# Two layer norms from one pass of statistics in the q, k, v stage of a three-block kernel

## The chip, the cores and the metric

The kernel runs on one core of a Trainium2 chip, in float32. The metric is the device time of one execution, in microseconds. A core has TensorE (matrix products into PSUM, profile name PE, with PEld for its weight loads), VectorE (DVE), ScalarE (ACT), GpSimd (POOL) and SyncE (SP, which here issues DMAs). They run side by side and wait for one another through semaphores.

## The reference

The input is x of 8 x 512 tokens with 128 channels, 4096 tokens in all. Three blocks follow each other, and the first and the third are the same computation:

```python
def _layernorm(x, axis=-1, eps=1e-05):
    m = jnp.mean(x, axis=axis, keepdims=True)
    v = jnp.var(x, axis=axis, keepdims=True)
    return (x - m) / jnp.sqrt(v + eps)

x = x + 0.5 * ffn(_layernorm(x))
x = x + attn(_layernorm(x))            # a recurrence over the tokens
x = x + 0.5 * ffn(_layernorm(x))

def ffn(x):                            # x is already normalized once
    x = x + _msa(_layernorm(x, ln1_w, ln1_b), w_qkv, w_proj)
    return x + _moe_mlp(_layernorm(x, ln2_w, ln2_b), gate_w, gate_b, w1, w2)
```

So at the start of `ffn` two layer norms stand one behind the other: z, the norm of x, which is kept for the residual, and the norm of z, which goes with weight and bias into the product with w_qkv (128 x 384, 16 heads of 8). If x has variance v along its channels, z has mean 0 and variance v / (v + eps).

## The kernel before, in words

`program` (L1949) runs `ffn`, the recurrence, `ffn` again and a last sum. Each `ffn` is four stages, one after another with a barrier of all engines between them: the q, k, v stage (`qkv_phase`, L290), attention, projection (with the second norm and the choice of experts) and experts.

The q, k, v stage works on 8 slices (SL) of 512 tokens; a slice is 4 tiles (ST) of 128 tokens by 128 channels, tokens on the partitions. `pipeline` (L75) lays the slices over each other: in step j an engine does part 0 for slice j, part 1 for slice j-1, and so on up to j-3. Steps 0 to 5 are written out, steps 6 and 7 are one turn of a hardware loop with the slice number in a register, steps 8 to 10 drain. Each engine's order is that in which its `step` lists the parts. Buffers come in pairs, by the parity of the slice.

For one slice:

- VectorE, `lna.center` (L132 to L140): sum over the channels (L134), mean (L136), x minus mean (L140). ScalarE, `squares` (L144): the squares of that. VectorE, `variance` (L151, L153): their sum, then scale and eps. GpSimd, `scale` (L159, L165): the power -0.5, then the multiply that writes z into `z_all`.
- The same four parts again, `lnb`, on z, one step later; GpSimd's multiply writes `zn`.
- TensorE transposes `zn` (L430); ScalarE applies weight and bias and writes `hT` (L384).
- TensorE multiplies: q and k (L420, with the weights stationary) and v (L424).
- ScalarE rounds q and k to a high part (L376), VectorE subtracts it to get the low part (L357), and SyncE stores both parts (L331), 512 KB for q and 512 KB for k per slice. ScalarE copies v into `v_all` (L390).

TensorE's order in a step is: q, k, v of slice j-3, then the transposes of slice j-2. ScalarE's is: high parts of j-3, Squares, `hT` of j-2, copy of v. VectorE's is: center of j, center of j-1, low parts of j-3, variance of j, variance of j-1. In the first `ffn` x is still being loaded, 256 KB a slice; VectorE waits for each.

The projection stage has a norm of another make, on VectorE alone apart from the power: `bn_stats` (L987) and `bn_aggr` (L995) for mean and variance, eps added (L1002), the power on GpSimd (L1140), and one tensor_scalar per tile that subtracts the mean and multiplies (L1008). The recurrence uses the same `LayerNorm` class (`lnr`, `gn`). In the expert stage VectorE copies weights (L1252) from an address that it reads into a register.

## Time and profile before

| | us |
|---|---|
| median of 3 runs | 1597.56 |
| lowest, highest | 1591.68, 1601.63 |
| the profiled execution | 1610.69 |
| its span, first to last instruction | 1608.9 |
| busy: TensorE, VectorE | 1292.8, 1121.5 |
| busy: ScalarE, GpSimd | 877.7, 698.0 |

All rows come from the one profiled execution. "Busy" adds up the durations of an engine's instructions over all stages; an engine that is busy for most of a stage sets its pace there, whatever its share of the whole span. In the timeline a row is a start, a duration, the engine, the line, and in brackets the idle time before it with what ended it; rows with a count (x4) are merged. An instruction may start before the one ahead of it has ended, so the pace of a row of them is read from start to start. Nearly all of the kernel's time lies in two attention stages, two expert stages and the recurrence; the q, k, v stages lie from 6 to 76 us and from 955 to 1028 us of the span.

### The profile page before, as it was taken

The numbers are of one execution on the slowest core, as the hardware profiler recorded it, in microseconds if no ns is written. First come the engines' busy times: TensorE is split into PE (matmuls) and PEld (weight loads), VectorE is DVE, ScalarE is ACT, GpSimd is POOL, SyncE is SP. The second block draws the span as 40 slices with busy tenths as digits, with TensorE's granted clock in tenths as the row PEclk, the third lists the DMA queues.
The fourth block names the chain that finished last, engine by engine and source line by source line (L and its number), as shares of the span: only waits on it lengthen the run. The fifth ranks groups of instructions, "written<-read, shape, count | busy, mean of one in ns | idle before, by whom it ended". The sixth has DMA issues, their size and how long they took to land. (4 is left out here: it accounts for less than half of the span.)

```text
span 1608.9 us, 39937 instructions
## 1 busy us (share of the span) xinstructions
PE 1292.8 (80%) x12720; PEld 732.9 (46%) x12721; DVE 1121.5 (70%) x1736; ACT 877.7 (55%) x1782; POOL 698.0 (43%) x817
## 2 busy tenths in 40 slices
PE   3579999999978397278788745489999999976693
PEld 2324444434458397125445433234444444476593
DVE  7678888888736232758788759588889888463232
ACT  3438888888841153224334314168888888820351
POOL 5433333333336365246566625513333333336462
PEclk9769999999975599589899858689999999965797
DMA  3421433211100121100000002512111111001224
GB/s 111 167 57 43 112 91 78 62 49 48 29 1 30 48 68 51 41 2 2 3 2 2 3 1 105 150 36 51 45 54 46 48 53 45 12 1 43 62 68 117
DMA packets 81641, 81.93 MB, mean 51 GB/s; under 512 B 16265, under 2 KB 53868, under 8 KB 81536
## 3 DMA queue, kind: packets, MB, share of 16 engines
q1 hardware_dynamic: 72704, 70.01, 15.6%
q0 software_dynamic: 4608, 8.44, 1.6%
q10 hardware_dynamic: 4224, 2.10, 0.4%
q8 instruction: 64, 1.05, 0.3%
q14 instruction: 41, 0.34, 0.1%
HBM read 50.56 MB, written 29.93 MB: 50 GB/s over the span
## 5 line engine op out<-in xcount | busy, mean ns | idle before, releaser
L795 DVE TENSOR_REDUCE maxima<-ps 128x2 f32<-128x1024 f32 x512 | 624.1, 1226 | 88.1 <-PE ps L624 83.1
L777 ACT ACTIVATE probs<-ps 128x512 f32<-128x512 f32 x1024 | 553.1, 593 | 87.0 <-PE ps L651 69.7
L624 PE MATMUL ps<-k_stack,q_stack 62*128 62x512 f32 x1024 | 385.8, 476 | 36.6 <-DMA k_stack<-k_split 25.5
L651 PE MATMUL ps<-q_stack,k_stack 64*128 64x512 f32 x1024 | 390.0, 459 | 0.3
L661 PE MATMUL ps<-probs,v_stack 128*32 128x256 f32 x4096 | 327.5, 392 | 1.1 <-ACT probs L777 1.0
L590 POOL TENSOR_TENSOR inv<-o_rows,minus_one 128x16 f32<-128x16 f32 x64 | 186.3, 2911 | 237.4 <-ACT o_rows L758 237.4
L624 PEld LDWEIGHTS ps<-k_stack,q_stack 62*128 62x128 f32 x1024 | 157.7, 193 | 229.7 <-issue 115.9
L651 PEld LDWEIGHTS ps<-q_stack,k_stack 64*128 64x128 f32 x1024 | 159.3, 186 | 17.0 <-issue 7.3
L661 PEld LDWEIGHTS ps<-probs,v_stack 128*32 128x32 f32 x4096 | 80.9, 108 | 171.7 <-issue 112.2
L1275 POOL DMA_INDIRECT expert_out<-yt,number x80 | 78.7, 984 | 69.0 <-issue 44.4
L1233 ACT ACTIVATE xT<-ps,ln_b,ln_w 128x128 f32<-128x128 f32 x80 | 36.6, 458 | 107.2 <-PE ps L1204 105.1
L1252 DVE COPY w_now<-w 128x512 f32 x80 | 34.4, 430 | 77.8 <-issue 41.6
L1210 PE MATMUL ps<-xT,w_now 128*128 128x128 f32 x640 | 88.4, 283 | 0.1
L1217 PE MATMUL ps<-w,hidT 128*128 x640 | 84.9, 276 | 0.0
L1210 PEld LDWEIGHTS ps<-xT,w_now 128*128 128x128 f32 x640 | 80.6, 198 | 0.4 <-issue 0.3
L583 POOL CAST neg_wide<-maxima 128x16 fp32r<-128x16 f32 x64 | 12.7, 198 | 155.1 <-DVE maxima L795 155.1
L1217 PEld LDWEIGHTS ps<-w,hidT 128*128 128x128 f32 x640 | 78.4, 193 | 0.1
L1133 POOL DMA_INDIRECT sorted<-rows,slot x64 | 62.2, 972 | 26.5 <-issue 16.4
L1238 ACT ACTIVATE hidT<-ps 128x512 f32<-128x512 f32 x80 | 47.8, 598 | 36.4 <-PE ps L1210 35.8
L1681 POOL TENSOR_TENSOR r_kx<-r_kx,r_k_factor 128x512 f32<-128x512 f32 x48 | 60.6, 1263 | 13.0 <-PE ps L1859 9.6
L1662 POOL TENSOR_TENSOR r_mixed<-r_shift,zT 128x512 f32<-128x512 f32 x40 | 57.1, 1436 | 19.0 <-DVE r_shift L1538 19.0
L420 PE MATMUL ps<-hT,w_qkv 128*128 128x512 f32 x64 | 44.7, 837 | 17.4 <-ACT hT L384 17.4
(215 smaller groups left out, 1843.8 us busy)
## 6 DMA issues: line engine op xcount, KB each, us to landing
q_stack<-q_split SPq DMA_DIRECT2D x256, 64.0 KB
k_stack<-k_split SPq DMA_DIRECT2D x512, 32.0 KB
q_split<-q_parts SPq DMA_DIRECT2D x16, 512.0 KB, 2.8
k_split<-k_parts SPq DMA_DIRECT2D x16, 512.0 KB, 3.6
xt<-sorted SPq DMA_DIRECT2D x80, 64.5 KB
w<-in_L_ffn_w SPq DMA_DIRECT2D x16, 256.0 KB, 3.0
rows<-expert_out SPq DMA_DIRECT2D x16, 256.0 KB, 3.2
x_all<-in_L_attn_x SPq DMA_DIRECT2D x8, 256.0 KB, 3.0
```

Of the source, the lines that this page charges most:

```text
L590: g_.tensor_tensor(inv[:], o_rows[:, :, :, DK], minus_one[:], ALU.pow).then_inc(inv_ready, 1)
L624: mm = t.matmul(psS[:, h, :], qs[g][score_rows(h), h // 2, u * P:(u + 1) * P], ks[g][score_rows(h), h // 2, :], start=True, stop=True)
L651: t.matmul(ring("e", u, n), ks[g][half(h), h // 2, u * P:(u + 1) * P], qs[g][half(h), h // 2, :], start=True, stop=True).then_inc(e_ready, 1)
L661: last = t.matmul(psO[VW * h:VW * (h + 1), here], vs[g][:, u, h, :], probs[u % 2][:, h, here], start=(u == 0 and part == 0), stop=(u == TP ...
L777: a.activation(probs[u % 2][:, h, :], ring("e", u, n), ACT.Exp, scale=float(DK) ** -0.5).then_inc(e_read, 1)
L795: v.tensor_reduce(maxima[i][:, :, pair, u:u + 1], psS[:, 2 * pair:2 * pair + 2, :], AX_X, ALU.max, negate=True).then_inc(s_read, 1)
L1133: pool.indirect_dma_start(xs, bass.IndirectOffsetOnAxis(ap=slot[:, i:i + 1], axis=0), rows[:, i, :], None).then_inc(scattered, 16)
L1210: last = t.matmul(psH[o][:, c * P:(c + 1) * P], w1_now[o][:, c * P:(c + 1) * P], xT[o][:], start=True, stop=True)
L1217: last = t.matmul(psY[i][:, 0:P], hidT[i][:, c, :], s["w2"][:, ds(second_expert, 1), c, :], start=(c == 0), stop=(c == HC - 1))
L1275: pool.indirect_dma_start(ys, bass.IndirectOffsetOnAxis(ap=number[out_slot][:], axis=0), yt[out_slot][:], None, bounds_check=TOK - 1, oob_ ...
L1662: g.tensor_tensor(mixed[f][:], shift[f % 2][:], x, ALU.add).then_inc(mixed_ready.sem, 1)
L1681: g.tensor_tensor(dst[:].rearrange("p (k m) -> p k m", m=m), src[:].rearrange("p (k m) -> p k m", m=m), k_factor[l][:].rearrange("p n two ...
```

## The change

In `qkv_phase` the two `LayerNorm` objects are replaced. VectorE takes mean and variance of each tile of x with `bn_stats` and `bn_aggr` (`moments_of`). From the variance v it writes two numbers per token: v + eps, and (1 + eps) v + eps^2, which is (v + eps) times (variance of z + eps). GpSimd raises both to the power -0.5 in one instruction of 128x8. One step later (`norm`) VectorE writes, for each of the four tiles, `zn` and `z_all`, both from x, with one tensor_scalar each: subtract the mean, multiply by the scale. ScalarE has no Squares any more, GpSimd no multiplies. TensorE waits for `normed` instead of for GpSimd.

```diff
-        lna = LayerNorm(nc, ctx, "lna", ST, EPS, bufs=2)
-        lnb = LayerNorm(nc, ctx, "lnb", ST, EPS, bufs=2)
+        stats, moments = sb("stats", [P, ST, 6]), sbs("moments", [P, ST, 2])
+        spread, scales, power = sbs("spread", [P, 2, ST]), sbs("scales", [P, 2, ST]), sb("power", [P, 2, ST])
...
+                def moments_of(j, i):
+                    after(vec, moments_made, j, 1)
+                    for q in range(ST):
+                        v.bn_stats(stats[:, q, :], x_all[:, j * ST + q, :] if isinstance(j, int)
+                                   else x_all[:, ds(j * ST + q, 1), :].rearrange("p a c -> p (a c)")).then_inc(stats_made, 1)
+                    after(vec, normed, j, 2)
+                    for q in range(ST):
+                        vec.wait_ge(stats_made, ST * j + q + 1)
+                        last = v.bn_aggr(moments[i][:, q, :], stats[:, q, :])
+                    last.then_inc(moments_made, 1)
+                    vec.wait_ge(moments_made, j + 1)
+                    after(vec, scales_made, j, 2)
+                    v.tensor_scalar(spread[i][:, 0, :], moments[i][:, :, 1], EPS, None, ALU.add)
+                    v.tensor_scalar(spread[i][:, 1, :], moments[i][:, :, 1], 1.0 + EPS, EPS * EPS, ALU.mult,
+                                    ALU.add).then_inc(spread_made, 1)
+
+                def norm(j, i):
+                    vec.wait_ge(scales_made, j + 1)
+                    after(vec, turned, j, 2)
+                    for q in range(ST):
+                        x = x_all[:, ds(j * ST + q, 1), :].rearrange("p a c -> p (a c)")
+                        z = z_all[:, ds(j * ST + q, 1), :].rearrange("p a c -> p (a c)")
+                        v.tensor_scalar(zn[i][:, q, :], x, moments[i][:, q, 0:1], scales[i][:, 1, q:q + 1],
+                                        ALU.subtract, ALU.mult)
+                        last = v.tensor_scalar(z, x, moments[i][:, q, 0:1], scales[i][:, 0, q:q + 1],
+                                               ALU.subtract, ALU.mult)
+                    last.then_inc(normed, 1)
...
-                        lna.center(vec, j, x_all[:, ds(j * ST, ST), :], i)
+                        moments_of(j, i)
                     if present(1):
-                        lna.wait_done(vec, j - 1)
-                        lnb.center(vec, j - 1, z_all[:, ds((j - 1) * ST, ST), :], o)
+                        norm(j - 1, o)
...
-                    if present(0):
-                        lna.variance(vec, j, i)
-                    if present(1):
-                        lnb.variance(vec, j - 1, o)
...
-                    if present(0):
-                        lna.squares(act, j, i)
-                    if present(1):
-                        lnb.squares(act, j - 1, o)
...
                     if present(0):
-                        lna.scale(pool, j, z_all[:, ds(j * ST, ST), :], i)
-                    if present(1):
-                        free = [] if isinstance(j, int) and j < 3 else [(turned, j - 2)]
-                        lnb.scale(pool, j - 1, zn[o][:], o, *free)
+                        pool.wait_ge(spread_made, j + 1)
+                        after(pool, normed, j, 2)
+                        g.tensor_tensor(scales[i][:], spread[i][:], power[:], ALU.pow).then_inc(scales_made, 1)
...
-                        lnb.wait_done(pe, j - 2)
+                        after(pe, normed, j, 2)
```

## Rows read from the trace of the kernel before

**Rows 1.** The page: busy time, share of the span and instructions of each engine.

```profile
PE 1292.8 (80%) x12720; PEld 732.9 (46%) x12721; DVE 1121.5 (70%) x1736; ACT 877.7 (55%) x1782; POOL 698.0 (43%) x817
```

**Rows 2.** Windows, second stage, one step: length, busy time by engine, clock, DMA, GB/s.

```profile
992.28:999.68 7.40, 5.19 (x17) 3.22 (x16) 7.19 (x13) 3.61 (x6) 4.04 (x5) 0.73 0.38 141
```

**Rows 3.** Groups of instructions of the second stage, 955 to 1024 us.

```profile
L165 POOL TENSOR_TENSOR z_all<-lna_centered,lna_rstd 128x512 f32<-128x512 f32 (+1 forms) x8 | 8.4, 1054 | 1.8 <-POOL lna_rstd L159 1.8
...
L136 DVE TENSOR_SCALAR lna_mean<-lna_total 128x4 f32<-128x4 f32 x8 | 6.3, 782 | 0.3
...
L136 DVE TENSOR_SCALAR lnb_mean<-lnb_total 128x4 f32<-128x4 f32 x8 | 5.6, 694 | 0.3
```

**Rows 4.** Timeline of the second stage: start, length, engine, line, operation, idle before.

```profile
955.35 0.69 DVE L134 TENSOR_REDUCE lna_total<-x_all 128x4 f32<-128x512 f32 x1 [1.29 <-PEq L63]
...
968.14 1.12 PE L430 MATMUL ps<-ident,zn 128*128 128x128 f32 x4 [14.80 <-POOL zn L165]
...
970.22 3.78 PE L420 MATMUL ps<-hT,w_qkv 128*128 128x512 f32 x4 [0.96 <-ACT hT L384]
...
976.51 1.98 PE L420 MATMUL ps<-hT,w_qkv 128*128 128x512 f32 x4 [0.87 <-ACT hT L384]
...
978.33 1.05 PE L424 MATMUL ps<-w_qkv,hT 128*128 128x128 f32 x8
...
989.48 0.68 DVE L357 TENSOR_TENSOR q_parts<-ps,q_parts 128x512 fp32r<-128x512 f32 x1
...
990.08 0.68 DVE L357 TENSOR_TENSOR k_parts<-ps,k_parts 128x512 fp32r<-128x512 f32 x1
...
1011.38 0.66 PE L430 MATMUL ps<-ident,zn 128*128 128x128 f32 x4 [2.74 <-POOL zn L165]
...
1012.91 3.78 PE L420 MATMUL ps<-hT,w_qkv 128*128 128x512 f32 x4 [0.87 <-ACT hT L384]
...
1020.01 1.99 PE L420 MATMUL ps<-hT,w_qkv 128*128 128x512 f32 x4 [0.87 <-ACT hT L384]
...
1023.38 0.37 SPq L331 DMA_DIRECT2D k_split<-k_parts  x1
```

**Rows 5.** Timeline of the first stage.

```profile
6.03 0.69 DVE L134 TENSOR_REDUCE lna_total<-x_all 128x4 f32<-128x512 f32 x1 [1.21 <-DMA x_all<-in_L_attn_x]
...
20.73 3.78 PE L420 MATMUL ps<-hT,w_qkv 128*128 128x512 f32 x4 [0.96 <-ACT hT L384]
...
27.30 1.98 PE L420 MATMUL ps<-hT,w_qkv 128*128 128x512 f32 x4 [0.87 <-ACT hT L384]
...
68.56 1.98 PE L420 MATMUL ps<-hT,w_qkv 128*128 128x512 f32 x4 [0.87 <-ACT hT L384]
```

**Rows 6.** Timeline of the projection stage, VectorE and GpSimd.

```profile
473.15 0.87 DVE L987 BATCH_NORM_STATS2 stats<-x 128x6 f32<-128x128 f32 x4
...
474.33 0.17 DVE L1002 TENSOR_SCALAR var<-moments 128x4 f32<-128x4 f32 x1
474.41 0.69 DVE L981 SCALAR_TENSOR_TENSOR x_all<-x,x_all 128x512 f32<-128x512 f32 x1
474.58 1.38 POOL L1140 TENSOR_TENSOR rstd<-var,power 128x4 f32<-128x4 f32 x1 [2.24 <-DVE var L1002]
475.01 1.11 DVE L1008 TENSOR_SCALAR rows<-x,moments,rstd 128x128 f32<-128x128 f32 x4
...
476.04 0.69 DVE L977 TENSOR_TENSOR x<-z_all,ps 128x512 f32<-128x512 f32 x1
```

**Rows 7.** Lines L159 and L1140: durations in ns, min/median/max, first and last start.

```profile
L159 POOL TENSOR_TENSOR gn_rstd<-gn_var,gn_power x8: 1637/1648/1650, 740.5 to 945.6; 128x8 f32<-128x8 f32 x8
...
L1140 POOL TENSOR_TENSOR rstd<-var,power x16: 1281/1404/1499, 471.1 to 1458.5; 128x4 f32<-128x4 f32 x16
```

**Rows 8.** DMA issues of the second stage: count, size, median us to landing.

```profile
k_split<-k_parts SPq DMA_DIRECT2D x8, 512.0 KB, 3.6
```

**Rows 9.** The page, costliest groups: a copy with an address from a register.

```profile
L1252 DVE COPY w_now<-w 128x512 f32 x80 | 34.4, 430 | 77.8 <-issue 41.6
```

More of the change, by code:

```diff
@@ L309, in sem @@
             return ctx.semaphore(name)
-        lna = LayerNorm(nc, ctx, "lna", ST, EPS, bufs=2)
-        lnb = LayerNorm(nc, ctx, "lnb", ST, EPS, bufs=2)
+        stats, moments = sb("stats", [P, ST, 6]), sbs("moments", [P, ST, 2])
+        spread, scales, power = sbs("spread", [P, 2, ST]), sbs("scales", [P, 2, ST]), sb("power", [P, 2, ST])
+        stats_made, moments_made, spread_made, scales_made, normed = (
+            sem("stats_made"), sem("moments_made"), sem("spread_made"), sem("scales_made"), sem("normed"))
+        power_set = sem("power_set")
         zn, hT = sbs("zn", [P, ST, P]), sbs("hT", [P, SW])
@@ L398, in step @@
                 def step(j, i, present):
-                    o = 1 - i
                     if present(0):
-                        lna.scale(pool, j, z_all[:, ds(j * ST, ST), :], i)
-                    if present(1):
-                        free = [] if isinstance(j, int) and j < 3 else [(turned, j - 2)]
-                        lnb.scale(pool, j - 1, zn[o][:], o, *free)
-                lna.start(pool)
-                lnb.start(pool)
+                        pool.wait_ge(spread_made, j + 1)
+                        after(pool, normed, j, 2)
+                        g.tensor_tensor(scales[i][:], spread[i][:], power[:], ALU.pow).then_inc(scales_made, 1)
+                g.memset(power[:], -0.5).then_inc(power_set, 1)
+                pool.wait_ge(power_set, 1)
                 g.memset(v_all[:, :, :, DK:], 1.0).then_inc(ones_set, 1)
-                pipeline(pool, SL, 1, step)
+                pipeline(pool, SL, 0, step)
             @block.tensor
```

## The prediction, made before the changed kernel was run

> **What bounds the kernel now.** I read the page's busy times first: TensorE is busy 80% and VectorE 70% of 1608.9 us, but over stages that differ [rows 1], and the change touches only the q, k, v stage, which runs twice. Of each run I read the timeline: in the second, VectorE's first reduction starts at 955.35 and the last store of k is issued at 1023.38, which is 68.0 us [rows 4]; in the first, VectorE starts at 6.03 and the last slice's q product at 68.56 [rows 5]. The store follows that product by 1023.38 - 1020.01 = 3.37 us, so the first run ends near 71.9. Together that is 134 us, or 8% of the span, and no more than this can be won. Then the windows of one step: in 7.40 us VectorE is busy 7.19, TensorE 5.19, ScalarE 3.61, GpSimd 4.04 [rows 2]. VectorE sets the pace. Some of its time is no work: the means, scalings of 4 numbers per partition, take 782 and 694 ns each, while the like operation on moments takes 0.17 us [rows 3, 6]. They stand beside GpSimd's 128x512 multiplies of 1054 ns [rows 3]. TensorE's 5.19 us are at a granted clock of 0.73 on average, thus partly at 1.2 and partly at 2.4 GHz [rows 2].
>
> **The change, part by part.** Removed per step: from VectorE four reductions, two means, two centerings and two variances (ten instructions), from ScalarE two Squares, from GpSimd one pow and two multiplies. Added on VectorE: four bn_stats, four bn_aggr, two small tensor_scalars, eight 128x128 tensor_scalars. GpSimd keeps one pow, now 128x8. The two subtractions for the low parts of q and k stay.
>
> VectorE's new step, by the projection stage, which does the same in the same shapes. Four bn_stats, four bn_aggr and one small tensor_scalar take 474.41 - 473.15 = 1.26 us, and each further small one 474.41 - 474.33 = 0.08: 1.34 for the moments [rows 6]. Four normalizing tensor_scalars with two per-partition operands take 476.04 - 475.01 = 1.03, eight of them 2.06 [rows 6]. The low parts go 990.08 - 989.48 = 0.60 apart, 1.20 for two [rows 4]. The sum is **4.60 us** against 7.40 [rows 2]. Bounds: if the eight did not overlap at all, 8 x 1.11/4 gives 2.22, and with a full 0.34 each 2.7, so a step is 4.6 to 5.3; below, nothing shown is shorter, and I leave 0.2 for it. I take 4.60, the same form on the same engine.
>
> TensorE is the next limit. Its step has a loop of its own: q, k, v, then the transposes of the next slice, ScalarE's hT, and the next q. At full clock q, k and v take 978.33 + 1.05 - 976.51 = 2.87 us, and from the transposes to the next q 1012.91 - 1011.38 = 1.53: **4.40 us** [rows 4]. At half clock the step is 1020.01 - 1012.91 = 7.10 [rows 4]. Which one holds? Before, the clock falls where TensorE has stood idle for 2 to 3 us a step (2.74 before the transposes at 1011.38, and the products at 1012.91 then take 3.78 instead of 1.98) [rows 4]. After, its idle time is about 0.9 us before q and little else, so I take full clock from the second slice on. One step at 7.10 instead would cost 2.7.
>
> The way in, second run. VectorE's moments of slice 0 end at 955.35 + 1.34 = 956.7; the pow starts 0.25 us after (474.58 - 474.33) [rows 6] and takes 1.65 [rows 7], until 958.6. Meanwhile VectorE does slice 1's moments, then waits 0.6 and writes both results by 960.7. The transposes start there and not at 968.14: 7.35 us earlier. To q(0) it was 970.22 - 968.14 = 2.08 [rows 4], so q(0) is at 962.9. From q(0) to q(1), with the clock still low in q(0), I keep the 976.51 - 970.22 = 6.29 [rows 4]: q(1) at 969.2. Then six steps of 4.40: q(7) at 995.6, and the last store 3.37 later at 998.9 instead of 1023.38: **24.4 us earlier**.
>
> Is VectorE in time? The low parts of slice 0 wait for ScalarE until about 967.5 and end at 968.7, and then each step is 4.60: the normalization of slice 7 ends at 968.7 + 4 x 4.60 + 3.40 = 990.5, and its transposes are due at 995.6 - 1.53 = 994.1. There are 3.6 us to spare, so even 5.3 a step costs under 1 us. The stores: two of 512 KB a step; one of k lands after 3.6 us [rows 8], and its buffer is written again two slices later. The latest, issued about 987.1, has landed at 990.7, and ScalarE wants it near 992.4: hidden, with 1.7 us of cover; without it a step would grow by what is missing. The pow of a slice has a whole step, 4.6 us, before VectorE wants it, and needs 0.25 + 1.65: hidden, with 2.7 us of cover.
>
> First run: the same 7.55 us from VectorE's start to q(0) give 6.03 + 7.55 = 13.6; q(0) to q(1) took 27.30 - 20.73 = 6.57 [rows 5]: 20.2; six steps: 46.6, against 68.56: **22.0 us earlier**. The load of x is no bound: it comes in two slices at a time, in less than a step.
>
> ScalarE loses its Squares, GpSimd its multiplies: neither is on the path, so 0, besides the port. The new waits on VectorE are for its own results (in the 1.26) and for the scales, behind which the low parts and all of the next step are queued; the cover is the 2.7 us. Step 6 and 7 run in a hardware loop, where each of the 12 new instructions takes one or two addresses from registers. The nearest row is a copy with an address from a register, with 41.6 us of issue idle in 80, 0.52 each, with a value load in it [rows 9]; below 0 nothing speaks. I take 0, since VectorE's queue runs ahead, and 0.52 for the range. Fewer semaphores to clear at the end may save some tenths: not counted.
>
> Sum: 24.4 + 22.0 = 46.4. The profiled execution took 1610.69 us (span 1608.9 and 1.8 around it), so it would be 1564.3; it lies 0.8% over the median 1597.56 of the runs, and against that the forecast is **1551.2**.
>
> **The port.** The row: VectorE's small means last until GpSimd's 1.05 us multiply is through, and that goes away with the multiplies [rows 3]. A pow does not do this: in the projection stage it runs from 474.58 for 1.38 us, while VectorE's four tensor_scalars start at 475.01 and keep their pace of 0.26 [rows 6]. The pow in turn varies from 1281 to 1499 ns [rows 7]. The Trainium skill, page "SBUF — State Buffer", section "Who interferes with whom", says that a VectorE tensor_scalar in a two-port mode and a GpSimd instruction lock each other out, the first to issue holding the pair for its whole length. By that rule, the trace agrees for the multiplies and not for the pow, and the new eight tensor_scalars would stand behind the pow in each step; what this would give is the first rival.
>
> **Rivals.**
> (1) The pow holds VectorE back for its 1.65 us a step. VectorE's step is 6.25: the low parts of slice 0 end at 972.0, the normalization of slice 7 at 972.0 + 25.0 + 5.05 = 1002.1, q(7) at 1003.7, 8.1 later than forecast; twice, 16.2: **1567**. For it: the multiplies do hold it. Against it: rows 6. 8%.
> (2) TensorE stays at half clock. q(7) at 962.9 + 7 x 7.10 = 1012.6, and a tail of 3.37 + 3.78 - 1.98 = 5.2: 5.6 us won; in the first run 3.4. Time **1589**. For it: the clock of 0.73 in a step that is 70% busy [rows 2]. Against it: the idle time goes. 6%.
> (3) The register addresses cost 0.52 each: 24 instructions, 12.5 less the 3.6 to spare, 9 a stage: **1569**. 6%.
> (4) The other side: the same place at a higher price. VectorE's sequencer stalls at each of the 24 instructions of the loop. It decides from (24.4 + 3.6)/24 = 1.17 us each; at 1.5 the stage loses 36 - 3.6 - 24.4 = 8 us and the first 10.4: **1616**, slower. For it only that VectorE now issues 20 instructions a step instead of 12; against it that the nearest row has 0.52. 3%. That the change doesn't do what it says has no case: the code leaves no second pass over z.
>
> **How the numbers follow.** The forecast has 77%; its own spread is one slow TensorE step a stage (+5), a faster first step (-4), and the 5 us by which runs differ: 1541 to 1561. The range reaches up to (1) and (3): 1541 to 1571, with (2) and (4) out, 9%, and the tails. A change of 1% (16 us) is about what can be told from none. Faster by more: 0.77 + 0.08 + 0.06 = 0.91; within: 0.06, case (2); slower: 0.03.
>
> **What would show it.** Steps of 4.4 to 4.7 us, with the last k store 43 to 46 us after VectorE's first bn_stats; the first transposes 5.4 us after it; TensorE waiting for hT by 0.9 us a step and hardly for VectorE; clock at 1 from the second slice; no small tensor_scalar above 0.2 us. Wrong would be: tensor_scalars of the norm above 0.5 us beside the pow (1), products of 3.8 us late in the stage (2), VectorE idle by issue in steps 6 and 7 (3, 4), or the attention stages taking longer than before.

## The result, and the profile after

The changed kernel takes 1550.81 us (median of 4 runs, 1547.22 to 1553.92) against 1597.8 for the kernel before (4 runs beside it, 1591.68 to 1601.63): a ratio of 0.9715, 95% interval 0.9682 to 0.9747. The forecast was 1551.2. The profiled execution took 1553.92 us, with a span of 1552.0.

First the page of the changed kernel, busy time, share and instructions of each engine, for [rows 1]:

```profile
PE 1284.2 (83%) x12720; PEld 729.3 (47%) x12721; DVE 1082.9 (70%) x1864; ACT 859.3 (55%) x1750; POOL 659.1 (42%) x767
```

VectorE has 128 instructions more and 39 us less to do, GpSimd 39 us less, ScalarE 18 us less. TensorE does the same work and shows 8.6 us less: in these stages four q and k matmuls take 3.78 us at half clock and 1.98 at full clock, and more of them now run at full clock.

Then one step of the second stage, from one group of `bn_stats` of VectorE to the next, for [rows 2]: length, busy time of PE, PEld, DVE, ACT and POOL with their instructions, granted clock, DMA share, GB/s.

```profile
951.21:955.79 4.58, 3.71 (x18) 2.31 (x17) 4.55 (x21) 2.61 (x5) 1.75 (x1) 1.00 0.59 229
```

A step is 4.58 us instead of 7.40. VectorE is busy for 4.55 of it, TensorE for 3.71, and the granted clock is 1.00, TensorE's 2.4 GHz level, where the step before had 0.73. At full clock both VectorE and TensorE are close to their limits here, which is the point of most experiments below.

The timeline of the second stage, for [rows 4] (start, duration, engine, line, and in brackets the idle time before it and what ended it). The lines are those of the changed kernel: L353 `bn_stats`, L372 and L374 the two normalizing tensor_scalars, L426 the pow, L452 the transposes, L442 the q product, L446 the v product.

```profile
928.88 0.88 DVE L353 BATCH_NORM_STATS2 stats<-x_all 128x6 f32<-128x128 f32 x4 [1.30 <-PEq L63]
...
934.25 1.12 PE L452 MATMUL ps<-ident,zn 128*128 128x128 f32 x4 [7.40 <-DVE z_all L374]
...
936.24 3.50 PE L442 MATMUL ps<-hT,w_qkv 128*128 128x512 f32 x4 [0.87 <-ACT hT L408]
...
941.94 1.99 PE L442 MATMUL ps<-hT,w_qkv 128*128 128x512 f32 x4 [0.87 <-ACT hT L408]
...
943.39 0.34 DVE L372 TENSOR_SCALAR zn<-x_all,moments,scales 128x128 f32<-128x128 f32 x1
943.64 1.75 POOL L426 TENSOR_TENSOR scales<-spread,power 128x8 f32<-128x8 f32 x1 [2.99 <-DVE spread L363]
943.65 0.34 DVE L374 TENSOR_SCALAR z_all<-x_all,moments,scales 128x128 f32<-128x128 f32 x1
943.76 1.05 PE L446 MATMUL ps<-w_qkv,hT 128*128 128x128 f32 x8
...
944.65 0.60 PE L452 MATMUL ps<-ident,zn 128*128 128x128 f32 x4
...
946.12 1.98 PE L442 MATMUL ps<-hT,w_qkv 128*128 128x512 f32 x4 [0.87 <-ACT hT L408]
...
946.64 0.87 DVE L353 BATCH_NORM_STATS2 stats<-x_all 128x6 f32<-128x128 f32 x4
...
951.21 0.87 DVE L353 BATCH_NORM_STATS2 stats<-x_all 128x6 f32<-128x128 f32 x4
...
967.01 1.99 PE L442 MATMUL ps<-hT,w_qkv 128*128 128x512 f32 x4 [0.87 <-ACT hT L408]
...
970.38 0.37 SPq L336 DMA_DIRECT2D k_split<-k_parts  x1
974.84 0.35 SPq L546 DMA_DIRECT2D q_stack<-q_split  x1
```

Read it from top to bottom. VectorE starts at 928.88, the first transposes start 5.37 us later (12.79 before), the first q product at 936.24, which is 7.36 after the start, the second at 941.94 and the third at 946.12. From here each q product starts 4.18 us after the one before it, up to the eighth at 967.01, and each names only ScalarE's `hT` as what it waited for, by 0.87 us. The last store of k is issued at 970.38, 41.50 us after VectorE's start, where it was 68.03. The rows at 943.39 to 943.65 also show a pow of 1.75 us beside the tensor_scalars of VectorE: they keep starting 0.26 apart. After the last store the first load of the attention stage is issued 4.46 us later; it was 4.72.

The first stage, for [rows 5], has the same steps:

```profile
5.73 0.87 DVE L353 BATCH_NORM_STATS2 stats<-x_all 128x6 f32<-128x128 f32 x4 [0.80 <-DMA x_all<-in_L_attn_x]
...
13.13 3.78 PE L442 MATMUL ps<-hT,w_qkv 128*128 128x512 f32 x4 [0.87 <-ACT hT L408]
...
19.56 1.99 PE L442 MATMUL ps<-hT,w_qkv 128*128 128x512 f32 x4 [0.87 <-ACT hT L408]
...
32.83 0.37 SPq L336 DMA_DIRECT2D k_split<-k_parts  x1
...
38.30 0.60 ACT L404 ACTIVATE k_parts<-ps 128x512 fp32r<-128x512 f32 x1 [0.26 <-PE ps L442]
...
48.01 0.37 SPq L336 DMA_DIRECT2D k_split<-k_parts  x1
52.16 0.35 SPq L546 DMA_DIRECT2D q_stack<-q_split  x1
```

From 5.73 to 48.01 is 42.28 us; before it was 65.90. The two rows at 32.83 and 38.30 are used below, where the stores are discussed.

Over both stages the profiled executions differ by 26.5 + 23.6 = 50.1 us up to the last stores, and by 0.3 a stage more up to the first loads of attention. That may be the fewer semaphores to clear there; no run shows it. The spans differ by more, 1608.9 - 1552.0 = 56.9, and the medians by less, 47.0. Two things explain that. The one profile of before fell high: its own time was 0.8% above the median. And everything outside the two stages, the same code in both kernels, took 1465.8 us in the profile of before and 1459.6 in that of after. Over all profiles of this study that remainder lay between 1451.5 and 1468.3, with no order by kernel but with one by chip: 1451.5 to 1459.0 on the chip where the kernel before took 1596.54 us, 1462.8 to 1468.3 where it took 1606.4, 1466.7 to 1467.7 where it took 1610.1. It differs mostly in the projection stages (73.5 to 83.9 us for the first of them). So stages are compared below by their own lengths, and totals only through the runs that share a chip.

### The profile page after: what moved, and what is told of

Same layout as the page of the kernel before. It is cut to its first block and busy times, and to the rows that moved or that the text cites. A ratio compares the mean times of both kernels' runs of the same rounds, so it can differ in the third digit from the quotient of the medians.

```text
span 1552.0 us, 39914 instructions
## 1 busy us (share of the span) xinstructions
PE 1284.2 (83%) x12720; PEld 729.3 (47%) x12721; DVE 1082.9 (70%) x1864; ACT 859.3 (55%) x1750; POOL 659.1 (42%) x767
## 3 DMA queue, kind: packets, MB, share of 16 engines
q8 instruction: 64, 1.05, 0.3%
## 5 line engine op out<-in xcount | busy, mean ns | idle before, releaser
L646 PE MATMUL ps<-k_stack,q_stack 62*128 62x512 f32 x1024 | 387.6, 478 | 35.6 <-DMA k_stack<-k_split 24.4
L1684 POOL TENSOR_TENSOR r_mixed<-r_shift,zT 128x512 f32<-128x512 f32 x40 | 56.9, 1431 | 18.0 <-DVE r_shift L1560 18.0
L1226 PE MATMUL ps<-ident,xt 128*128 128x128 f32 x80 | 23.3, 292 | 44.2 <-DMA xt<-sorted 44.1
```

The costliest lines, as they stand in the source:

```text
L646: mm = t.matmul(psS[:, h, :], qs[g][score_rows(h), h // 2, u * P:(u + 1) * P], ks[g][score_rows(h), h // 2, :], start=True, stop=True)
L1684: g.tensor_tensor(mixed[f][:], shift[f % 2][:], x, ALU.add).then_inc(mixed_ready.sem, 1)
```

## The experiments

"Stage" is the time from VectorE's first instruction of a q, k, v stage to the issue of its last k store, second stage first. The stage lengths of a row come from one profile. "us" is the median of the runs: 4 for the first rows of before and changed, 5 for "changed, again" and the two rows with ratios of their own, and a single run for all others. "Before there" is the median of 9 runs of the kernel before on the same chip (of 4 for 1597.8).

| kernel | second | first | T(0) | us | before there |
|---|---|---|---|---|---|
| before | 68.03 | 65.90 | 12.8 | 1597.8 | |
| before, again | 66.72 | 64.41 | 12.8 | 1608.7 | 1610.1 |
| changed | 41.50 | 42.28 | 5.4 | 1550.81 | 1597.8 |
| changed, again | 42.69 | 42.48 | 5.4 | 1561.5 | 1606.4 |
| changed, third time | 42.87 | 42.41 | 5.4 | 1563.73 | 1610.1 |
| transposes twice | 46.20 | 45.74 | 5.4 | 1570.64 | 1606.4 |
| one more VectorE instruction | 44.46 | 47.83 | 5.4 | 1569.79 | 1606.4 |
| transposes before v | 39.73 | 40.36 | 5.4 | 1554.04 | 1606.4 |
| two passes, VectorE writes | 52.13 | 52.14 | 9.5 | 1574.3 | 1596.54 |
| one pass, GpSimd writes | 42.42 | 43.04 | 5.9 | 1547.51 | 1596.54 |
| before, VectorE writes | 62.97 | 62.87 | 13.1 | 1592.38 | 1596.54 |
| transposes before v, `zn` first | 39.74 | 40.44 | 4.4 | 1546.05 | 1596.54 |
| one pass, GpSimd writes, transposes before v | 38.00 | 38.01 | 5.9 | 1550.53 | 1610.1 |

T(0) is the start of the first transposes after VectorE's first instruction. My theory, called A where an expectation has letters: the way to the first transposes got shorter by 7.4 us (7.2 in the first stage), and after it the loop of TensorE and ScalarE (q, k, v, transposes, `hT`, q) sets the pace. The rivals: VectorE's step, 4.57 us long, sets it; the gain comes from VectorE writing instead of GpSimd, and not from the one pass; or part of the gain is given back in the stages that follow. A further one, that the gain lies in how the statistics are taken (`bn_stats` and `bn_aggr` instead of sums, centering and Squares) and not in taking them once, has no run of its own, but two of the runs below differ by that.

**The changed kernel again**, no edit, five runs on another chip.

> The changed kernel once more, unaltered, for a tighter ratio. In its first profile the two q, k, v stages (VectorE's first instruction to the first load of the attention stage) are 46.4 and 46.0 us long against 70.3 and 72.8 before, so they give back 23.9 and 26.8, together 50.7 us, while the medians differ by 47.0. Theory A: the stages are worth 50.7 us in every execution and the rest is scatter of the other stages: a ratio of 1 - 50.7/1597.8 = 0.968, with the interval reaching below 0.970. Theory B: about 4 us of it come back in a later stage: a ratio of 0.971 or above, with 0.968 outside.

Measured: 1561.5 against 1606.4, ratio 0.9714, interval 0.969 to 0.9737. The ratio holds on a chip that is 0.5% slower for the kernel before and 0.7% for the changed one. By the letters of the expectation this is B's sign, a ratio of 0.971 or above with 0.968 outside; whether B's cause is there, 4 us paid back in a later stage, is taken up with the last profiles below. The second stage took 42.69: its steps are 4.18 again, but from q(0) to q(1) it was 6.88 us where the first profile had 5.70. In both the product q(0) starts at half clock (3.78 us for four, and 3.50 in the first profile, where the clock rose within it). The moment of the rise is the 1.2 us between 41.50 and 42.69.

**The transposes twice.** TensorE does the four transposes of a slice two times; the result is the same.

```diff
-                        for q in range(ST):
+                        for q in list(range(ST)) * 2:
                             last = t.transpose(psT[i][:, q * P:(q + 1) * P], zn[i][:, q, :], s["ident"][:])
```

> TensorE transposes each slice twice, 0.45 us more a step at full clock. Stage length is from VectorE's first bn_stats to the issue of the last k store, 41.5 us in the second stage now. Theory A (the loop TensorE, hT on ScalarE, TensorE sets the pace, VectorE has room): seven slices pay, the first at half clock, so 45.0 to 45.6. Theory B (VectorE's 4.57 us a step set the pace): 41.5 to 42.

Measured: stages of 46.20 and 45.74, 3.5 and 3.3 us over those of the changed kernel on that chip, and 1570.64 against 1561.5. That is above A's 45.0 to 45.6, which was reckoned from 41.5 and not from the 42.69 of that chip, and far from B's. From the second slice on q products start at 952.02, 956.64, 961.26 and 965.87: a step of 4.62 where it was 4.18, so 0.44 of work on TensorE costs 0.44 in each step. Work on TensorE is on the path in every step. From v to the transposes it is 0.89 still, and from there to q 1.91 instead of 1.47. Six such steps are 2.6 us; the first slice, whose transposes run at half clock, takes 2.84 from T(0) to q(0) where it was 1.98, and that is the rest of the 3.5.

**One more instruction on VectorE**, a subtraction of 128x512 behind the norm, whose result nobody reads.

```diff
                         norm(j - 1, o)
+                        after(vec, spare_made, j, 2)
+                        x = x_all[:, ds((j - 1) * ST, ST), :]
+                        v.tensor_tensor(spare[:], x, x, ALU.subtract).then_inc(spare_made, 1)
```

> VectorE gets one more 128x512 subtraction of 0.61 us a slice, behind the norm, whose result nobody reads. Theory A (TensorE's loop sets the pace, VectorE is 3.1 us ahead at the last slice: the norm of slice 7 ends at 962.4, its transposes start at 965.6): seven of them are 4.3, so 1.2 to 2 us show: second stage 42.7 to 43.5 instead of 41.5. Theory B (VectorE sets the pace): eight show in full, 46.4.

Measured: 44.46 in the second stage, between the two expectations, and 47.83 in the first, above both. VectorE's step is 5.17 (low parts of q at 961.49, 966.66, 971.83). In the second stage the q products still start 4.18 apart up to q(5) (955.54, 959.72, 963.90, 968.08), then 4.81 and 5.04: there ScalarE waits 1.63 and 2.01 us for the q store of two slices before, and TensorE 1.72 for `hT`. So VectorE's longer step does reach the end, but by way of the stores that its late low parts delay; the transposes themselves wait for VectorE once, by 0.41 us, and the last ones not at all. The first stage shows this at its worst, and neither theory had it. Its timeline:

```profile
35.89 0.37 SPq L337 DMA_DIRECT2D q_split<-q_parts  x1
...
41.09 0.60 ACT L408 ACTIVATE q_parts<-ps 128x512 fp32r<-128x512 f32 x1 [4.24 <-DMA q_split<-q_parts]
...
42.83 0.77 ACT L412 ACTIVATE hT<-ps,ln_b,ln_w 128x512 f32<-128x512 f32 x1
...
43.65 3.78 PE L446 MATMUL ps<-hT,w_qkv 128*128 128x512 f32 x4 [3.10 <-ACT hT L412]
```

The q store issued at 35.89 has to land before ScalarE may write that buffer again, and it took 5.2 us. ScalarE works in order, so `hT` of the next slice, ready to be made, is queued behind that wait of 4.24 us; TensorE stands idle for 3.10, and its clock is down afterwards: the four q products at 43.65 take 3.78 us, where they took 1.98 above. A later low part means a later store, and the store means a later `hT`. The long landing is no accident of this run: the k store of slice 3 in the first stage took 5.2 to 5.3 us in all three profiles of the changed kernel, where it cost nothing, and 5.76 here. Each time the trace has a 16 KB packet of an instruction queue among the store's packets (at 37.93 here, for 0.95 us); that it causes the delay is likely and not tested. There is thus a third limit a little above the two that I had: store, landing, ScalarE.

**The transposes before v.** In a step TensorE does q, k, then the transposes of the next slice, then v, so that ScalarE makes `hT` beside v.

```diff
                     if present(3):
-                        ...            # v of slice j-3
                     if present(2):
                         ...            # transposes of slice j-2
+                    if present(3):
+                        ...            # v of slice j-3
```

> TensorE transposes the next slice before the v product, so that ScalarE's hT runs beside v and no longer between two slices. Theory A (that loop sets the pace now): TensorE's step falls from 4.18 to about 3.5, VectorE's 4.57 becomes the bound, and the last slice follows its norm (33.5 us into the stage) by 1.5 + 3.4: second stage 38.4 to 38.9 instead of 41.5, about 6 us for both. Theory B (VectorE sets the pace already): 41.5 as now.

Measured: 39.73 and 40.36, that is 3.0 and 2.1 less than the changed kernel there, and 1554.04 against 1561.5. The direction is that of A, the size is not: 38.4 to 38.9 was expected. The timeline of the second stage shows why:

```profile
954.37 0.37 SPq L336 DMA_DIRECT2D q_split<-q_parts  x1
...
954.97 0.37 SPq L336 DMA_DIRECT2D k_split<-k_parts  x1
...
955.32 1.98 PE L442 MATMUL ps<-hT,w_qkv 128*128 128x512 f32 x4
...
957.15 0.60 ACT L404 ACTIVATE q_parts<-ps 128x512 fp32r<-128x512 f32 x1 [1.17 <-DMA q_split<-q_parts]
...
958.37 0.66 PE L447 MATMUL ps<-ident,zn 128*128 128x128 f32 x4 [1.06 <-DVE z_all L374]
958.42 0.60 ACT L404 ACTIVATE k_parts<-ps 128x512 fp32r<-128x512 f32 x1 [0.67 <-DMA k_split<-k_parts]
...
959.07 0.78 ACT L408 ACTIVATE hT<-ps,ln_b,ln_w 128x512 f32<-128x512 f32 x1
...
959.89 1.99 PE L442 MATMUL ps<-hT,w_qkv 128*128 128x512 f32 x4
```

The q products at 944.43, 947.77 and 951.11 (not printed) start 3.34 apart, faster than VectorE's 4.57. The surplus is used up after slice 4: the transposes of slice 5 wait 0.71 us for VectorE (at 953.80, not printed), those of slice 6, at 958.37, wait 1.06, ScalarE waits 1.17 and 0.67 us for stores to land (the q store of 954.37 is released at 957.15, after 2.78 us; the k store of 954.97 at 958.42, after 3.45). With TensorE out of the way, VectorE's pace and the stores are the next limits, and they lie close. In the first stage the long landing of slice 3 shows too: ScalarE waits 3.01 us for it, one step is 6.19 us, and the stage is 0.6 longer than the second.

**Two passes, both results on VectorE.** The changed kernel with its one pass undone: GpSimd's pow gives the scale of the first norm, VectorE writes z, takes `bn_stats` and `bn_aggr` of z one step later, waits for a second pow and writes `zn` from z.

```diff
+                def moments2_of(j, i):
+                    ...
+                        v.bn_stats(stats2[:, q, :], z_all[:, ds(j * ST + q, 1), :].rearrange("p a c -> p (a c)"))...
+                    ...
+                    v.tensor_scalar(spread2[i][:], moments2[i][:, :, 1], EPS, None, ALU.add).then_inc(spread2_made, 1)
...
                         norm(j - 1, o)
+                        moments2_of(j - 1, o)
+                    if present(2):
+                        norm2(j - 2, i)
```

> Undoes the one pass alone: mean and variance of z are taken from z again with bn_stats and bn_aggr, a second pow makes its scale, and VectorE still writes both results. VectorE's step is then 2 x 1.26 + 2 x 1.03 + 1.20 = 5.8 us and the first transposes come 4.1 us later. Theory A (VectorE becomes the bound above 4.2 to 4.6 us a step): second stage, first VectorE instruction to last k store, 48 to 50 us instead of 41.5. Rival (the gain is all from GpSimd's multiplies and the port): 41.5 to 43.

Measured: T(0) at 9.5, as expected; stages of 52.13 and 52.14, 2 to 4 above the expectation; 1574.3 against 1596.54. Its timeline, second stage (L413 is the low part of q, once a step):

```profile
958.71 0.68 DVE L413 TENSOR_TENSOR q_parts<-ps,q_parts 128x512 fp32r<-128x512 f32 x1
...
964.48 0.68 DVE L413 TENSOR_TENSOR q_parts<-ps,q_parts 128x512 fp32r<-128x512 f32 x1
```

VectorE's step is 964.48 - 958.71 = 5.77 us. This kernel gets 12 to 16 us a stage of the 23 to 25, and the one pass the other 10 (52.13 against 42.35 and 52.14 against 42.39, the changed kernel's means over three profiles): 1.2 us of VectorE a step and 4.1 us of way in.

**One pass, GpSimd writes.** The other half undone: VectorE takes the moments and subtracts the mean, GpSimd raises to the power and does both multiplies.

```diff
+                    v.tensor_tensor(centered[i][:], x_all[:, ds(j * ST, ST), :], wide(moments[i][:, :, 0]),
+                                    ALU.subtract).then_inc(centered_made, 1)
...
-                        norm(j - 1, o)
...
+                        g.tensor_tensor(zn[i][:], centered[i][:], wide(scales[i][:, 1, :]), ALU.mult)
+                        g.tensor_tensor(z_all[:, ds(j * ST, ST), :], centered[i][:], wide(scales[i][:, 0, :]),
+                                        ALU.mult).then_inc(normed, 1)
```

> Undoes the writing on VectorE alone: statistics in one pass as changed, VectorE centers x once (0.61 us), and GpSimd writes zn and z with two multiplies of 1.05 us behind its pow. VectorE's own work is 3.2 us a step, GpSimd's about 4.2 (1.7 + 0.2 + 2.1 + 0.2). Theory A (the one pass is what counts): second stage 41.5 to 44 us. Rival (the port): VectorE's small tensor_scalars wait for the multiplies, and the multiplies for VectorE's centering, which drives GpSimd's step past 5: 47 us or more.

Measured: 42.42 and 43.04, and 1547.51 against 1596.54 (0.969, from one run of it). That is the changed kernel, and within A's 41.5 to 44. In the second stage:

```profile
952.21 0.68 DVE L370 TENSOR_TENSOR centered<-x_all,moments 128x512 f32<-128x512 f32 x1
...
952.46 1.33 POOL L435 TENSOR_TENSOR zn<-centered,scales 128x512 f32<-128x512 f32 x1 [0.27 <-POOL scales L431]
...
955.98 1.98 PE L453 MATMUL ps<-hT,w_qkv 128*128 128x512 f32 x4 [0.87 <-ACT hT L413]
...
960.16 1.98 PE L453 MATMUL ps<-hT,w_qkv 128*128 128x512 f32 x4 [0.87 <-ACT hT L413]
```

TensorE keeps its step of 960.16 - 955.98 = 4.18; GpSimd has about 3.9 us of work a step and is under it. One of its multiplies takes 1.33 us where it stands beside VectorE's centering (up to 1.46 elsewhere in the run), and it is hidden. That VectorE writes both results is no part of the gain. With two passes GpSimd's multiplies held VectorE up [rows 3]; with one, the small instructions of VectorE fall beside the pow: 26 of the 32 small tensor_scalars of both stages do, and none takes over 0.17 us.

**The kernel before, with only the multiplies on VectorE.**

```diff
-                        lna.scale(pool, j, z_all[:, ds(j * ST, ST), :], i)
+                        lna.power_(pool, j, i)
...
                     if present(1):
+                        lna.scale_on_vector(vec, j - 1, z_all[:, ds((j - 1) * ST, ST), :], o)
                         lna.wait_done(vec, j - 1)
...
+                    if present(2):
+                        after(vec, turned, j, 4)
+                        lnb.scale_on_vector(vec, j - 2, zn[i][:], i)
```

> The kernel before, with only the two multiplies moved from GpSimd to VectorE (centered times scale, 128x512, 0.61 us each); reductions, Squares and the second pass stay. VectorE gains the 1.14 us a step that its means waited for GpSimd and pays 1.22. Theory A (VectorE's sum sets the pace): second stage 67 to 70 us against 68.0 before, nothing won. Rival (the port waits were the cost, and the way through GpSimd): below 62.

Measured: 62.97 and 62.87, below my 67 to 70 and above the rival's 62; 1592.38 against 1596.54. In the second stage, VectorE and a pow of GpSimd:

```profile
970.03 0.68 DVE L134 TENSOR_REDUCE lna_total<-x_all 128x4 f32<-128x512 f32 x1
...
970.37 1.01 POOL L159 TENSOR_TENSOR lnb_rstd<-lnb_var,lnb_power 128x4 f32<-128x4 f32 x1
...
970.74 0.17 DVE L136 TENSOR_SCALAR lna_mean<-lna_total 128x4 f32<-128x4 f32 x1
...
977.20 0.68 DVE L134 TENSOR_REDUCE lna_total<-x_all 128x4 f32<-128x512 f32 x1
```

The mean at 970.74 takes 0.17 us, the same instruction that took 782 ns on average [rows 3]: with no multiply of GpSimd beside it, it doesn't wait, though a pow of 1.01 us runs beside it from 970.37. The step is 977.20 - 970.03 = 7.17 instead of 7.40: two multiplies of 0.68 came in and the two means gave up more than that. In the steady steps of before they took 0.99 to 1.02 and 0.90, and I had worked with the means over all slices, 0.78 and 0.69. The rest of the 3 to 5 us a stage (1.5 to 4 against the second profile of before) is not settled; the clock falls in both kernels in the middle of the stage, at other slices.

Between this kernel and the one with two passes both statistics are taken twice and VectorE writes both results; what differs is the make, `bn_stats`, `bn_aggr` and tensor_scalars with a mean and a scale instead of sums, centering, Squares on ScalarE and multiplies. The stages differ by 62.97 - 52.13 = 10.8 and 62.87 - 52.14 = 10.7 us, and T(0) by 3.6. So the make of the statistics is worth as much as the one pass.

**The transposes before v, and `zn` written first.** As above, and VectorE writes the four tiles of `zn` with a semaphore of their own, and only then `z_all`.

> The changed kernel with two orders altered: TensorE's transposes before its v product, and VectorE's four writes of zn ahead of its four of z, with a semaphore of their own, so that the transposes can start 1.0 us earlier. Theory A (the loop of TensorE and ScalarE, then VectorE, set the pace): first transposes 4.3 us after VectorE's first instruction instead of 5.4, second stage 37.4 to 38 us instead of 41.5, both stages 7 to 8 us shorter; ratio to the kernel before 0.964 to 0.967. Theory B (VectorE already bound): 40.5 to 41.5 a stage.

Measured: T(0) at 4.35 to 4.39, as expected, but stages of 39.74 and 40.44, between the two expectations, and not less than 39.73 and 40.36 without the new order. The end of the second stage:

```profile
949.97 0.37 SPq L337 DMA_DIRECT2D q_split<-q_parts  x1
...
952.76 0.60 ACT L408 ACTIVATE q_parts<-ps 128x512 fp32r<-128x512 f32 x1 [1.56 <-DMA q_split<-q_parts]
...
955.35 1.98 PE L446 MATMUL ps<-hT,w_qkv 128*128 128x512 f32 x4 [1.27 <-ACT hT L412]
```

The last transposes wait for nobody here. What holds q(7) is the store issued at 949.97: ScalarE waits 1.56 us for it, then 0.67 for that of k, and `hT` stands behind both. VectorE makes the low parts after all eight writes in either order, so their stores go out no earlier: this one 30.99 us into the stage, against 30.98 for the same one without the new order. The microsecond won on the way in is lost there. The total, five runs: 1546.05 against 1596.54, 0.9672, interval 0.9652 to 0.9692. That is better than the changed kernel by 0.4%, with intervals that overlap a little; the ratio expected was 0.964 to 0.967.

**The kernel before again**, no edit, one profile.

> The kernel before, profiled once more, since all stage lengths of before come from one execution. The changed kernel's two profiles have q, k, v stages (to the first load of attention) of 46.4 + 46.0 and 46.6 + 47.1 us, before 70.3 + 72.8. Theory A (the stages' length is a property of the kernel): 143 us for both within 2. Theory B (the one profile had them long by chance, which is why the medians moved by only 45 to 47 us): 138 to 140.

Measured: stages of 66.72 and 64.41, 1.3 and 1.5 under those of the profile that the prediction used. Up to the first loads of attention, as the expectation has it, they are 71.43 and 68.82, together 140.25: nearly B's 138 to 140, and outside A's 143 within 2. The two profiles of before differ by 2.8 us in these stages, and the forecast was built on the longer one. The difference lies in the clock. TensorE's q products in the drain of the second stage:

```profile
1010.44 3.63 PE L420 MATMUL ps<-hT,w_qkv 128*128 128x512 f32 x4 [0.87 <-ACT hT L384]
...
1016.27 1.98 PE L420 MATMUL ps<-hT,w_qkv 128*128 128x512 f32 x4 [0.87 <-ACT hT L384]
```

They start 5.83 us apart. In the first profile the last two were 1020.01 - 1012.91 = 7.10 apart [rows 4]. Before the change the clock falls and rises within the stage at moments that differ from run to run.

**Both findings together**: GpSimd writes, and the transposes come before v.

> Both findings together: one pass of statistics, z and zn written by GpSimd from an x that VectorE has centered, and TensorE's transposes ahead of its v product. VectorE's work is 3.2 us a step, TensorE's 3.5, GpSimd's pow and two multiplies 3.99 by its rows. Theory A (now GpSimd sets the pace at about 4.0, and the stores of the low parts go out early, since VectorE no longer lags): second stage, first VectorE instruction to last k store, 37.4 to 38.8 us against 41.5 in the changed kernel and 39.7 with the order alone; ratio to before 0.962 to 0.967. Theory B (the landing of the stores, some 3 us, in ScalarE's turn between two slices of one buffer, sets the pace): 39.5 to 41.

Measured: 38.00 and 38.01, as A has it, and over five runs 1550.53 against 1610.1, ratio 0.9626, interval 0.9608 to 0.9643. It beats the kernel before and the changed one, whose interval beside two other series of before begins at 0.9682 or 0.969. In the second stage:

```profile
951.40 1.64 POOL L431 TENSOR_TENSOR scales<-spread,power 128x8 f32<-128x8 f32 x1
...
953.30 1.04 POOL L435 TENSOR_TENSOR zn<-centered,scales 128x512 f32<-128x512 f32 x1 [0.27 <-POOL scales L431]
...
953.94 1.98 PE L453 MATMUL ps<-hT,w_qkv 128*128 128x512 f32 x4
...
955.30 1.64 POOL L431 TENSOR_TENSOR scales<-spread,power 128x8 f32<-128x8 f32 x1
...
957.28 1.98 PE L453 MATMUL ps<-hT,w_qkv 128*128 128x512 f32 x4
...
959.20 1.64 POOL L431 TENSOR_TENSOR scales<-spread,power 128x8 f32<-128x8 f32 x1
...
963.20 0.66 PE L458 MATMUL ps<-ident,zn 128*128 128x128 f32 x4 [0.39 <-POOL z_all L436]
```

GpSimd's pow starts at 951.40, 955.30 and 959.20: its step of 3.90, with 1.64 for the pow and two multiplies of 1.04, is the longest of all, while TensorE does 957.28 - 953.94 = 3.34 in the middle of the stage. By the last slice TensorE has caught up: its transposes at 963.20 wait 0.39 us for GpSimd's result. VectorE is busy 3.22 of the 3.90. Whoever goes on from here has GpSimd's pow to look at.

**The changed kernel a third time**, one profile, on the chip of the last two.

> The changed kernel, profiled a third time on the chip of the run of before beside it. Theory A: stages of 46 to 47 us each, so 49 to 51 us less than before's two, and whatever else the totals differ by lies in the projection and expert stages with their indirect DMAs, in either direction. Theory B (something later pays back 4 us): those other stages longer than before's in every profile of the changed kernel.

Measured: 42.87 and 42.41, and 1563.73 against 1610.1, a ratio of 0.971. With it the stages of the changed kernel are 42.35 and 42.39 on average over three profiles, and those of before 67.4 and 65.2 over two: 25.0 + 22.8, with the ends of the stages 48.3 us. The medians of the runs give 47.0 (interval 40.4 to 50.8, from the ratio) and 44.9 on the second chip. The stages are 47.32 and 46.57 up to the first loads, against A's 46 to 47, and together 46.4 us less than those of before on that chip; the 49 to 51 expected had the long profile in it. Outside the stages this kernel took 1467.7 us and before again 1466.7, on one chip, and in the first pair of profiles it was 1459.6 against 1465.8. So B's sign, the other stages longer each time, is missing, and no more than about 1 us can have been given back later. That answers the ratio of the second chip too: 1606.4 less 46.4 to 48.3 is a ratio of 0.970 or 0.971.

## Why the prediction was right

- **What bounds it, and how much can be won.** Right: VectorE set 7.40 us a step, and the gain is inside the stages.
- **VectorE's step.** 4.60 forecast, 4.57 measured, from rows of the projection stage. The four edits of which it was made up hold one by one: the port wait goes with the multiplies (small tensor_scalars 0.16 to 0.17 us), the eight normalizing ones start 0.26 apart.
- **The way in.** First transposes 5.35 after VectorE's start forecast, 5.37 measured; q(0) at 7.55 against 7.36. About 0.1 of that is a slip: from 968.14 to the forecast 960.7 is 7.44 and not 7.35. From q(0) to q(1) I kept 6.29; it was 5.70 once and 6.88 and 7.07 in the other two profiles (mean 6.55), and 6.43 to 6.63 in the first stages for a forecast of 6.57. This step was right in the mean only, and it holds most of what stages vary by.
- **TensorE's step.** The one mis-sized term: "4.40 us" is 4.18 in every step after q(1). I had summed v's 1.05 us to its end, while the transposes start 0.89 after v's start (944.65 - 943.76); q to v is 1.82, and transposes to q 1.47 and not 1.53: 1.82 + 0.89 + 1.47. Six steps of 0.22 are 1.3 us a stage, more than the 0.7 by which each stage won more than forecast. My signs had this too high as well: the last k store 43 to 46 us after the first `bn_stats`, where it came after 41.5 to 42.9, and steps of 4.4 to 4.7, which only VectorE's 4.57 met.
- **Full clock from the second slice.** Right: the q products take 1.98 or 1.99 us from q(1) on, in both stages, and the window shows 1.00. TensorE idle for 0.87 us a step does not bring the clock down; 3.10 did, in the kernel with one more VectorE instruction.
- **The tail** was 970.38 - 967.01 = 3.37, as forecast.
- **Is VectorE in time.** 3.6 us to spare were forecast; the norm of slice 7 ended at 962.4 and its transposes started at 965.55, 3.1. That VectorE with 4.57 a step isn't the bound at 4.18 a step for TensorE is only due to this start; the stage has eight slices and not thirty. The transposes twice confirm it, and the one more VectorE instruction shows what lies behind it.
- **The stores.** Cover of 1.7 us forecast. The q store of slice 4 was issued at 959.87 and ScalarE wrote the buffer again at 964.00, 4.13 us later; k had 4.39. Against this kernel's median landings of 2.7 and 3.4 that is 1.4 and 1.0 us: hidden, but by less. The closest place is in the first stage, and I had no term for it: the k store of slice 3, issued at 32.83, landed after 5.30 us at 38.13, and ScalarE wrote its buffer again at 38.30. It was hidden by 0.2 us, in the other two profiles by 0.4 and 0.3. With a VectorE step 0.6 longer it was not.
- **No issue stalls by registers.** Right: VectorE keeps 4.57 in the steps of the hardware loop too.
- **After the stages.** Attention, from its first load to the projection stage, took 388.6 and 387.6 us in the kernel before and 388.2 and 390.6 in the changed one; in the second pair 387.1 and 389.8, against 388.4 and 388.5. It did not get longer beyond its scatter, as forecast.
- **Sum.** 24.4 and 22.0 forecast for the stages; 25.0 and 22.8 measured over the profiles, and 0.5 for the ends that I had not counted. Against the one profile that the forecast started from they are 26.5 and 23.6. The medians' 47.0 is within 0.6 of the 46.4.

The rivals. (1) The pow holds VectorE back: false. This group of the changed kernel (count, least, median and greatest duration in ns) has all 16 pows and all 64 tensor_scalars that write `zn`:

```profile
L426 POOL TENSOR_TENSOR scales<-spread,power x16: 1630/1753/1838, 7.2 to 957.3; 128x8 f32<-128x8 f32 x16
...
L372 DVE TENSOR_SCALAR zn<-x_all,moments,scales x64: 336/341/375, 9.0 to 961.9; 128x128 f32<-128x128 f32 x64
```

Beside a pow of up to 1838 ns no tensor_scalar took more than 375. The rule of the Trainium skill's page "SBUF — State Buffer", section "Who interferes with whom", that a two-port tensor_scalar and a GpSimd instruction lock each other out for a whole instruction, holds here for GpSimd's multiplies beside VectorE's small tensor_scalars (0.17 us became 0.8 to 1.0), and not for its pow. Other runs tell that it is the pow, and not only the form of those tensor_scalars (two operands per partition): the mean (L136), held to 0.8 to 1.0 us beside multiplies in the kernel before, takes 0.17 beside a pow in all 14 cases in the kernel before with VectorE writing. Whether a multiply would hold a tensor_scalar with two operands per partition, no run shows. (2) Half clock, (3) and (4) issue stalls: none was seen. The forecast's number came from the right steps; it was helped by two errors that point in opposite directions, TensorE's step (1.3 us a stage) and the first profile of before being long (0.7 us a stage against the mean of its two). And that 1551.2 and 1550.81 agree to 0.4 us is luck: the interval of the gain is 10 us wide, and another chip gave 44.9 us for the same change.

What the study adds to the forecast is which part of the change earns it. The one pass earns about 10 of the 23 to 25 us a stage. The make of the statistics earns 10.7 or 10.8 more, between two kernels that both take them twice. GpSimd's multiplies out of VectorE's way, alone, were worth 1.5 to 5. VectorE writing both results is no part of it: with GpSimd writing them the stages are the same, and with the order of TensorE changed as well they are shorter by 4.4 us.

## What to carry to other kernels

When a norm follows a norm, its variance can be worked out from the first's, and what that saves is not only the second reduction but its whole turn through the pipeline. Taking mean and variance with `bn_stats` and `bn_aggr` was worth as much here, between two kernels that both take the statistics twice. Build the new step of the slowest engine from rows of the same shapes elsewhere in the trace, then build the step of the next engine from start to start (never from ends, since these overlap), and count who is ahead and by how much over the number of slices that there are. And when the slowest engine has been relieved, look again at where each part stands: here one exchange of two groups on TensorE gave another 2 to 3 us a stage, and 4 to 5 with the multiplies on GpSimd, which by then had little to do and was the better place for them.

## What the runs showed of the hardware

- A pow of 128x8 on GpSimd (1630 to 1838 ns) leaves VectorE's 128x128 tensor_scalars at 336 to 375 ns with starts 0.26 apart, while a 128x512 multiply on GpSimd holds a 128x4 tensor_scalar of 0.17 us for up to 1.0. Beside a pow of 128x4 that same tensor_scalar keeps its 0.17.
- The same 512 KB store from SBUF to DRAM released its waiter after 2.78 us in one place and after 5.2 in another; in the latter its last packets moved at 26 GB/s for 2 us, after about 390 in the 2 us before. The long one comes back at the same slice of the first stage in every profile of the changed kernel (5.2 to 5.3 us). I had taken one landing of 3.6 us for all.
- ScalarE's wait for a store is a wait of everything behind it: 4.24 us there became 3.10 of idle TensorE, and those a lower clock, with q products of 3.78 us instead of 1.98.
- When TensorE's clock rises in the first product of a stage, 3.50 or 3.78 us for the same four matmuls, differs from run to run, and moves the second product by up to 1.4 us.
